# Last stage of a graph network on one core: radial network and layer norm for two items at once, and a new order of the work in each slot

## What is computed

```
emb = radial_embedding(edge_weight)                      # 8 values per edge
h = silu(emb @ w0 + b0); h = silu(h @ w1 + b1)           # 64 wide
w = (h @ w2 + b2).reshape(-1, 4, 32)                     # per edge
xs, xv = x[src] @ W_up                                   # gathered rows, scalar and vector part
m = products of w, xs, xv and the edge direction         # 2 x 128 per edge
out = segment_sum(m, dst) @ W_out                        # summed over equal dst (edges are sorted)
x = layernorm(x + out / 16)                              # 128 wide
```

## Time and profile before

| | us |
|---|---|
| device time, median of 3 runs | 5631.95 (5623.3 to 5632.62) |
| the profiled execution | 5625.35 |
| its span | 5623.7 |
| the changed stage, first gather to the end | 4252.1 to 5623.7 |
| PE busy in the whole span | 3333.1 (59%) |
| DVE | 3545.2 (63%) |
| ACT | 3016.3 (54%) |
| POOL | 3641.2 (65%) |

### The profile page before, as it was taken

The page is one execution under the profiler, slowest core; times in us unless marked ns, Lnnn a source line. Parts: engine busy times, 40 slices in busy tenths (PEclk is TensorE's granted clock), DMA queues, the critical chain, the costliest instruction groups (busy, mean ns, idle before and its releaser), DMA issues. The chain is left out here.

```text
span 5623.7 us, 74514 instructions
## 1 busy us (share of the span) xinstructions
PE 3333.1 (59%) x15856; PEld 2601.5 (46%) x15856; DVE 3545.2 (63%) x12659; ACT 3016.3 (54%) x7426; POOL 3641.2 (65%) x3635
## 2 busy tenths in 40 slices
PE   3536555356626662646666466679886666666664
PEld 3536555344414441545555354445554444444443
DVE  6686555578877774757888733347774555555554
ACT  0106666378848881864555433335554555555554
POOL 5767777677757773877555177767774555555554
PEclk9999999999968886987777688865567777777777
DMA  2337777678827772655555488866672111112111
GB/s 73 77 82 239 238 240 244 160 224 251 250 76 223 226 226 78 205 177 158 168 167 164 150 228 225 225 187 206 205 212 68 52 54 55 54 54 54 55 54 47
DMA packets 819909, 861.98 MB, mean 153 GB/s; under 512 B 159976, under 2 KB 593741, under 8 KB 819099
## 3 DMA queue, kind: packets, MB, share of 16 engines
q1 hardware_dynamic: 703528, 673.45, 38.6%
q0 software_dynamic: 112896, 179.36, 13.5%
q10 hardware_dynamic: 3314, 7.36, 0.4%
HBM read 494.56 MB, written 370.75 MB: 154 GB/s over the span
## 5 line engine op out<-in xcount | busy, mean ns | idle before, releaser
L2151 POOL DMA_INDIRECT out_dram<-mss_o,kept_scat_idx x392 | 389.8, 994 | 452.2 <-ACT mss_o L1433 349.7
L1592 POOL DMA_INDIRECT att_xs<-t_t,kept_idx_a x392 | 370.2, 944 | 259.6 <-ACT att_xw L1719 137.9
L1895 POOL DMA_INDIRECT gs_xs<-t_t,kept_idx_b x392 | 369.8, 943 | 232.5 <-issue 118.9
L1035 POOL DMA_INDIRECT t_alpha<-gsm_raw,gsm_edge_idx x392 | 386.0, 985 | 165.6 <-issue 118.6
L2159 POOL DMA_INDIRECT mss_xs<-t_x,kept_idx_a x392 | 375.9, 959 | 168.1 <-issue 117.6
L534 POOL DMA_INDIRECT sort_xd<-in_x_dram,kept_dst_idx x392 | 379.6, 968 | 140.3 <-issue 118.5
L2015 POOL DMA_INDIRECT gs_xs<-t_z,kept_idx_a x392 | 379.5, 968 | 140.2 <-issue 119.2
L1025 POOL DMA_INDIRECT gsm_raw<-t_al,kept_idx_b x392 | 379.2, 967 | 124.6 <-issue 118.9
L1227 PE MATMUL gsm_hp<-kept_w,gsm_zT 128*128 128x128 f32 x1568 | 256.2, 313 | 342.3 <-ACT gsm_zT L1093 342.0
L536 POOL DMA_INDIRECT sort_xs<-in_x_dram,kept_src_idx x392 | 378.6, 966 | 119.5 <-issue 118.6
L216 PE MATMUL gs_tp<-kept_ident,gs_xs 128*128 128x128 f32 x784 | 277.7, 371 | 251.0 <-DMA gs_xs<-t_t,kept_idx_b 151.5
(11 more groups left out here) (561 smaller groups left out, 12127.7 us busy)
## 6 DMA issues: line engine op xcount, KB each, us to landing
t_t<-sort_o SPq DMA_DIRECT2D x66, 792.0 KB
t_x<-gsm_o SPq DMA_DIRECT2D x196, 264.0 KB
sort_x<-in_x_dram SPq DMA_DIRECT2D x66, 768.0 KB
gsm_x<-t_t SPq DMA_DIRECT2D x196, 256.0 KB
t_z<-gsm_z SPq DMA_DIRECT2D x196, 256.0 KB
out_dram<-gsm_o SPq DMA_DIRECT2D x196, 256.0 KB, 3.0
t_t<-l_o SPq DMA_DIRECT2D x49, 528.0 KB, 3.1
att_own<-t_t SPq DMA_DIRECT2D x49, 528.0 KB
```

Source lines behind the costliest of these rows:

```text
L1035: pool.indirect_dma_start(T["alpha"], bass.IndirectOffsetOnAxis(edge_idx[:, c:c + 1], 0), raw[:, c, :], None).then_inc(scattered[u], 16)
L1592: pool.indirect_dma_start(xs[q % RING][:, j, :], None, T["t12"][0:EP + N], bass.IndirectOffsetOnAxis(K["idx_a"][:, c:c + 1], 0)).then_inc( ...
L1895: pool.indirect_dma_start(xs[u][:, j, :], None, T["t12"], bass.IndirectOffsetOnAxis(K["idx_b"][:, c:c + 1], 0)).then_inc(gathered[u], 16)
L2151: pool.indirect_dma_start(T["out"], bass.IndirectOffsetOnAxis(K["scat_idx"][:, c:c + 1], 0), o[u][:, j, :], None, bounds_check=N - 1, oob_ ...
```

## The change

A step with `every` = 2 works on a pair of items in every second slot. The core of the diff (full functions of one kind are left out where only the counting of the semaphores is different):

```diff
-SCATTER_LAG = 15
+FINAL_LAG = 18
...
-        y = [sb(f"y{u}", [P, 4, D]) for u in range(BUFS)]
+        y = [sb(f"y{k}", [P, 2 * 4, D]) for k in range(3)]
-        h1 = [sb(f"h1{v}", [P, 2, P]) for v in range(2)]
-        h2 = [sb(f"h2{v}", [P, 2, P]) for v in range(2)]
+        h1, h2 = sb("h1", [P, 4, P]), sb("h2", [P, 4, P])
-        hp, wp = ps("hp", [P, 4, P]), ps("wp", [P, 4, D])
+        rad, wp = ps("rad", [P, 4, P]), ps("wp", [P, 4, D])
...
         @block.sync
+            for q in range(ITEMS):
+                if q >= 6:
+                    sp.wait_ge(applied, q - 5)
+                sp.dma_start(y[q // 2 % 3][:, 4 * (q % 2):4 * (q % 2) + 4, :], ...)
+                if q % 2 == 1:
+                    sp.wait_ge(y_loaded[q // 2 % 3], 32 * (q // 6) + 32)
...
         @block.tensor
+            def radial_first(k):
+                if k >= 1:
+                    pe.wait_ge(h2_done, k)
+                for pair in range(4):
+                    mm = pe.matmul(rad[:, pair, :], K["m0g"][:, pair, :], K["emb"][:, k * P:(k + 1) * P], ...)
+                mm.then_inc(h1_ready, 1)
+            def radial_second(k):
+                pe.wait_ge(h1_done, k + 1)
+                pe.matmul(rad[:]..., K["m1"][:], h1[:]..., start=True, stop=True).then_inc(h2_ready, 1)
+            def radial_third(q):
+                pe.wait_ge(h2_done, q // 2 + 1)
...
-            pipeline(pe, (radial_second, 1), (turn_x, 1), (turn_back, 9), (project, 3), (radial_third, 2), (radial_first, 0), (reduce, 7), (turn_sums, 5))
+            in_slots((radial_third, 3, 1, ITEMS), (turn_x, 1, 1, ITEMS), (turn_sums, 5, 1, ITEMS), (radial_second, 2, 2, ITEMS // 2),
+                     (reduce, 7, 1, ITEMS), (turn_back, 9, 1, ITEMS), (project, 3, 1, ITEMS), (radial_first, 1, 2, ITEMS // 2))
...
         @block.scalar
+            def radial_one(k):
+                act.wait_ge(h1_ready, k + 1)
+                if k >= 1:
+                    act.wait_ge(h2_ready, k)
+                act.activation(h1[:], rad[:], ACT.Silu, bias=K["mb0"][:, 0:1]).then_inc(h1_done, 1)
+            def radial_two(k):
+                act.wait_ge(h2_ready, k + 1)
+                ...
+                act.activation(h2[:], rad[:], ACT.Silu, bias=K["mb1"][:, 0:1]).then_inc(h2_done, 1)
+            def root(p):
+                act.wait_ge(measured, p + 1)
+                act.activation(sd[p % 2][:], var[p % 2][:], ACT.Sqrt, ...).then_inc(rooted, 1)
+            def apply(q):
+                act.wait_ge(scale_made, p + 1)
+                if q >= BUFS:
+                    act.wait_ge(scattered[q % BUFS], 64 * (q // BUFS))
...
-            pipeline(act, (radial_two, 1), (copy_x, 2), (radial_one, 0), (copy_msg, 6), (lambda t, u: norm_root(norm, act, t, u), 11), (scale_x, 0),
-                     (lambda t, u: norm_apply(norm, act, t, u, scattered, 64), 12))
+            in_slots((copy_x, 2, 1, ITEMS), (copy_msg, 6, 1, ITEMS), (radial_one, 2, 2, ITEMS // 2), (root, 13, 2, ITEMS // 2),
+                     (scale_x, 0, 1, ITEMS), (apply, 14, 1, ITEMS), (radial_two, 2, 2, ITEMS // 2))
...
         @block.vector
-            pipeline(dve, (scan, 8), (messages, 4), (keep, 3), (combine, 10), (lambda t, u: norm_scale(norm, dve, t, u), 11))
+            in_slots((scan, 8, 1, ITEMS), (combine, 10, 1, ITEMS), (messages, 4, 1, ITEMS), (keep, 3, 1, ITEMS), (count, 10, 1, ITEMS),
+                     (measure, 12, 2, ITEMS // 2), (scale, 13, 2, ITEMS // 2))
```

More of the change, by code:

```diff
@@ L2163, in _ @@
+                if q >= FINAL_LAG:
+                    scatter(q - FINAL_LAG)
             for u in range(BUFS):
@@ L2167, in _, with turn_x @@
         def _(pe):
-            def turn_x(t, u):
-                pe.wait_ge(scaled[u], t + 1)
-                wait_item(pe, x_copied, t, u, 1)
+            def turn_x(q):
+                pe.wait_ge(scaled, q + 1)
+                if q >= 1:
+                    pe.wait_ge(x_copied, q)
                 for j in range(4):
[L2172 to L2177, removed]
-                for j in range(4):
-                    mm = pe.matmul(up[:, j, :], xsT[u % 2][:, j, :], K["wup"][:], start=True, stop=True)
-                mm.then_inc(up_ready[u], 1)
@@ L2182, in turn_sums, with project @@
-            def turn_sums(t, u):
-                pe.wait_ge(msg_ready[u], t + 1)
-                wait_item(pe, msg_copied, t, u, 1)
+                    tr = pe.transpose(xtp[:, j, :], xk[q % 2][:, j, :], K["ident"][:])
+                tr.then_inc(x_turned, 1)
+            def project(q):
+                pe.wait_ge(x_copied, q + 1)
+                if q >= 1:
+                    pe.wait_ge(msg_ready, q)
+                for j in range(4):
+                    mm = pe.matmul(up[:, j, :], xsT[q % 2][:, j, :], K["wup"][:], start=True, stop=True)
+                mm.then_inc(up_ready, 1)
@@ L2185, in turn_sums @@
+            def turn_sums(q):
+                pe.wait_ge(msg_ready, q + 1)
+                if q >= 1:
+                    pe.wait_ge(msg_copied, q)
                 for a in range(parts):
                     for j in range(4):
[L2187 to L2192, removed]
-                for a in range(parts):
-                    mm = pe.matmul(rp[:], K["wout"][:, a, :], mT[u % 2][:, a, :], start=(a == 0), stop=(a == parts - 1))
-                mm.then_inc(reduced_t[u], 1)
@@ L2209, in radial_second @@
[L2209 to L2219, removed]
@@ new lines, in scale_x, with copy_x, copy_msg @@
+                ac.then_inc(scaled, 1)
+            def copy_x(q):
+                act.wait_ge(x_turned, q + 1)
+                if q >= 2:
+                    act.wait_ge(up_ready, q - 1)
+                act.copy(xsT[q % 2][:], xtp[:]).then_inc(x_copied, 1)
+            def copy_msg(q):
+                act.wait_ge(sums_turned, q + 1)
+                if q >= 2:
+                    act.wait_ge(reduced_t, q - 1)
+                for a in range(parts):
+                    ac = act.copy(mT[q % 2][:, a, :], tp[:, a].rearrange("p j i -> p (j i)"))
+                ac.then_inc(msg_copied, 1)
@@ new lines, in combine, with count @@
+            def combine(q):
+                rows = y[q // 2 % 3][:, 4 * (q % 2):4 * (q % 2) + 4, :]
+                dve.wait_ge(reduced, q + 1)
+                dve.wait_ge(y_loaded[q // 2 % 3], 32 * (q // 6) + 32)
+                dve.tensor_tensor(rows, rows, op[:], ALU.add).then_inc(combined, 1)
+            def count(q):
+                dve.wait_ge(combined, q + 1)
+                for g in range(4 * (q % 2), 4 * (q % 2) + 4):
+                    bn = dve.bn_stats(stats[q // 2 % 2][:, g, :], y[q // 2 % 3][:, g, :])
+                bn.then_inc(counted, 1)
@@ new lines, in measure @@
+            def measure(p):
+                v = p % 2
+                dve.wait_ge(counted, 2 * p + 2)
+                even, odd = stats[v][:, :, 0:3], stats[v][:, :, 3:6]
+                dve.tensor_tensor(diff[v][:], even[:, :, 1], odd[:, :, 1], ALU.subtract)
+                dve.tensor_tensor(total[v][:], even[:, :, 1], odd[:, :, 1], ALU.add)
+                link(dve.tensor_tensor(var[v][:], even[:, :, 2], odd[:, :, 2], ALU.add))
+                link(dve.scalar_tensor_tensor(out=diff[v][:], in0=diff[v][:], scalar=D / 4.0, in1=diff[v][:], op0=ALU.mult, op1=ALU.mult))
+                dve.tensor_tensor(var[v][:], var[v][:], diff[v][:], ALU.add).then_inc(measured, 1)
@@ new lines, in scale, with keep @@
+            def scale(p):
+                v = p % 2
+                dve.wait_ge(rooted, p + 1)
+                if p >= 2:
+                    dve.wait_ge(applied, 2 * p - 2)
+                link(dve.reciprocal(rs[v][:], sd[v][:]))
+                dve.scalar_tensor_tensor(out=nb[v][:], in0=total[v][:], scalar=-0.5, in1=rs[v][:], op0=ALU.mult, op1=ALU.mult).then_inc(scale_made, 1)
+            def keep(q):
+                dve.wait_ge(wp_ready, q + 1)
+                if q >= 2:
+                    dve.wait_ge(msg_ready, q - 1)
+                dve.tensor_tensor(wt[q % 2][:], wp[:], K["mb2"][:].unsqueeze(1).broadcast_to([P, 4, D]), ALU.add).then_inc(wt_ready, 1)
```

171 lines of the change are left out of this document (81 added, 90 removed).

## The result

The changed kernel takes **5290.41 us** (median of 4 runs, 5285.87 to 5297.62) where the kernel before takes 5632.28 on the same chip: ratio 0.9396 (0.9380 to 0.9412), 342 us less. The forecast was 5282. The profiled execution took 5290.85, its span 5288.9.

The account below looks back on a forecast made before the run. It took ACT and PE taking turns, 13.51 us a slot, as the bound, moving to POOL at 10.25. Start to 4350.5, 820.0 for 80 slots, 92.9 and 10.0 gave span 5273.4; plus 1.65 and 6.6, 5282 us; range 5250 to 5410.

Parts of the forecast that it names:

- The round of ACT and PE: Last stage, old kernel: ACT and PE alternate between `copy_x` and `radial_one`, 5.4 + 8.0 us and small change, 13.5 a slot.
- DVE and PE only at the end of the stage, 9.82 us: End of old stage: round from `combine` to `combine`, 9.82 us, because `reduce` stood behind `turn_back` and `scan` waited for it.
- The ceiling moves to POOL: Steady slots of the new stage: POOL's four scatters and four gathers set 10.25 us a slot for 13.51.
- The pairing: Steps for two items at once: ACT falls from 7.9 to 6.2 us a slot, DVE to 6.5 busy.
- PE's clock: the rival: New steady slots: PE becomes the bound through a low clock, 11.5 us a slot, 5387, or 5454 at 1.2 GHz; chance 0.13.
- The rows of the second convolution: Evidence for the PE clock rival: another stage, PE busy 125.9 of 140 us, granted a clock of only 0.56.
- POOL's lead of four slots: New stage: `gather` and `scatter` wait for ACT's steps four slots back, so POOL may be four slots ahead and does not wait.
- SP's loads at "nothing": SP's residual loads: issued two slots before use; the new wait holds only SP's own next load, costing nothing.
- to POOL's slot 18: Fill from the first gather at 4252.1 to POOL's first slot with scatters, at 4350.5.
- 80 slots: Steady part with gathers and scatters: 80 slots, 820.0 us, to 5170.5.
- last 18 items' scatters: End of the stage: 18 items' scatters, 4 x 1.29 us each, 92.9 us without POOL waiting, to 5263.4.
- The 6.6 us added for the distance between the profiled run and the median: Last term: the profiled execution was 6.6 us under the median of the runs, added to 5275 to give 5282.

Follow-up runs that it names:

- The order alone: Changed kernel with the pairing undone (radial network, root and norm for one item in each slot), new order kept: 5285.07 us, 0.9374 of the kernel before.
- the kernel of the order alone with the product in place: Changed kernel without pairing, first weighted product written over the scalar part in PSUM and read there by the 384-column product: 5273.38 us, 0.9364.

## Why the prediction held, step by step

- **The bound before: right, but one of two.** The round of ACT and PE is in the rows. "POOL, DVE and the DMA engines are carried along" was wrong for DVE: its wait of 511.8 us for the root is longer than the 475 us of `radial_one`, and the round through it is as long as the first. The forecast looked at DVE and PE only at the end of the stage, 9.82 us, where `scan` does wait for `reduce`; in a steady slot the round goes through ACT's root. By these rows a change that broke one round alone would have brought next to nothing; no run tried that. The new order breaks both: no ACT step ahead of the root waits for PE's work of the same slot, and `combine` stands right behind `scan`. So the forecast was not hurt, which was luck as far as this second round goes.
- **The ceiling moves to POOL: right.** Forecast 10.25 us a slot; 10.28 without the long product's collisions, 10.46 with them. A scatter fewer is worth nearly what it costs; less work on ACT and DVE (pairing, tables) is worth nothing.
- **The pairing: sizes near, worth nothing.** ACT 506.88 / 800 x 10.46 = 6.6 us a slot for 6.2; 88 table loads for about 98; the SiLU of 512 columns 0.69 for 0.65; DVE 6.6 for 6.5. The forecast listed these as if they made room that was needed. The order alone runs with 8.05 us on ACT.
- **PE's clock: the rival did not come.** PE works 602.46 / 800 x 10.46 = 7.9 us a slot (6.1 to 8.4 in the forecast) at a granted clock of 0.89, for 0.75 before, with all of its 16 transposes a slot; with one scatter it is 1.00. The rows of the second convolution did not carry over.
- **POOL's lead of four slots: right and needed**, as a lag of 14 shows. PE's wait for `radial_two` was forecast at some 3 us in odd slots: 87.8 us in 35 times, 2.5.
- **SP's loads at "nothing": the time is right, the reason is not.** DVE stands 219.7 us in 39 times for residual rows. `combine` waits for both halves of a pair, and the load of the second half is issued only one slot before, not two. DVE's slack hides it (6.6 of 10.46 us).
- **The sum**, by its own terms:

| term | forecast | measured | difference |
|---|---|---|---|
| first gather | 4252.1 | 4258.00 | +5.9 |
| to POOL's slot 18 | 98.4 | 90.7 | -7.7 |
| 80 slots | 820.0 | 837.1 | +17.1 |
| last 18 items' scatters | 92.9 | 92.7 | -0.2 |
| to the span's end | 10.0 | 10.4 | +0.4 |
| span | 5273.4 | 5288.9 | +15.5 |

The first term lies in earlier stages (4252 to 4264 in the profiles of this study). It and the second, +5.9 and -7.7, nearly cancel, by luck. The second: the fill is already POOL's, 18 x 5.04 us, which stood in the forecast as a bound; 7.3 us a slot for DVE in slots 8 to 14 was wrong. **The mis-sized term is the third**: "I take 10.25" is a value between two sums, both from a kernel where POOL waited each slot. Eight undisturbed instructions take 10.28, and the first scatter of four is the longest (1.02 us) without a pause before it too; the long instructions are +0.18 us a slot, and taking their cause away gives 10.28 and 5272.5 to 5274.8 us. The 6.6 us added for the distance between the profiled run and the median happened to cancel a good part of the miss of 15.5: this profile lay at the median itself, and 8.4 us are left.

## What to carry to other kernels

In a pipeline of slots with single banks, write down every round (who reads a bank, who refills it, what stands between in each list) for a steady slot, and start from the longest wait of every engine, not from that of one. Two rounds can share a stretch and be equally long, as here; work taken away counts only as far as it lies on each of them: 2.57 us of table loads brought 0.85. Read first and write last, and give the in-order queue at the end a lead of several slots; only then ask whether less work is worth anything, by taking work away from the engine that would be the bound. When POOL issues back to back, look for its instructions that are longer than the others and at what DVE starts just before them.

## What the runs showed of the hardware

An indirect DMA that POOL starts while DVE multiplies two SBUF operands of 128x384 (0.56 us) ends 1.4 to 1.5 us after the product's start: started 0.1 us into the product it lasts 1.28 us (35 cases in the changed kernel, means), at 0.2 us 1.21, at 0.3 us 1.11, at 0.4 us 1.01, and at 0.5 us 0.97, as alone. One that starts just before the product is not longer (4348.68, 0.08 us before it: 0.95 us). It looks as if most of a DMA's issue (1.4 - 0.56 = 0.85 us) could begin only when the product was over. With one operand in PSUM it lasts 0.94 to 1.02 us at every distance, as alone. In the kernel before only 3 of the 98 products had an instruction of POOL start within them, in the changed one 81.

The shorter products of two SBUF operands (0.29 us) do the same on a smaller scale. 0.29 + 0.85 is 1.14 us, so only an instruction that starts in about their first 0.15 us can be longer. In the kernel of the order alone with the product in place, 14 started 0.05 to 0.10 us after one of them, and lasted 1.03 to 1.09 us; one of these, behind the scatter that went ahead of it:

```profile
4482.30 0.98 POOL L2151 DMA_INDIRECT out_dram<-mss_o,kept_scat_idx  x1 [0.30 <-issue]
...
4483.53 0.29 DVE L2303 TENSOR_TENSOR mss_tmp<-mss_tmp 128x128 f32<-128x128 f32 x1
4483.59 1.09 POOL L2151 DMA_INDIRECT out_dram<-mss_o,kept_scat_idx  x1 [0.30 <-issue]
```

Those that start 0.2 us after such a product show nothing (76 behind L2303 in the changed kernel, mean 1.00, longest 1.04 us).

The Trainium skill, "SBUF — State Buffer", section "SBUF: two separate sides", says that DVE and GpSimd (POOL) share a pair of ports that is locked for a whole instruction, also by a DVE operation with two SBUF inputs against GpSimd work that reads SBUF, and that the one that comes second blocks. The trace agrees where POOL comes second, for the long product and the short ones, and the PSUM operand is the cure that this rule suggests. The other side is not seen: 45 long products of the changed kernel began while an instruction of POOL ran, and none lasted over 0.58 us.
